# A first expert layer whose second biases move from TensorE to VectorE, with the shared expert's transposition ahead of the third down projection

## The reference, cut to what matters

```python
xf = x.reshape(-1, h)
scores = jax.nn.sigmoid(xf @ gate_w.T + gate_b)
top_scores, top_idx = jax.lax.top_k(scores, TOP_K)
top_scores = top_scores / (top_scores.sum(-1, keepdims=True) + 1e-06)
comb = (jax.nn.one_hot(top_idx, E, dtype=xf.dtype) * top_scores[..., None]).sum(1)
hdn = jax.nn.gelu(jnp.einsum('th,ehf->etf', xf, w1) + b1[:, None, :], approximate=False)
y = jnp.einsum('etf,efh->eth', hdn, w2) + b2[:, None, :]
routed = jnp.einsum('te,eth->th', comb, y)
shared = (jax.nn.gelu(xf @ sw1 + sb1, approximate=False) @ sw2 + sb2) * 0.1
return (routed + shared).reshape(b, s, h)
```

## Time and profile before

| | |
|---|---|
| timed runs | 260.24, 260.38, 261.11 us; median 260.38 |
| profiled execution, its own time | 262.31 us |
| its span, first to last instruction | 260.5 us |
| TensorE, weight loads | 232.2 us (89%), 142.5 us (55%) |
| VectorE, ScalarE | 169.2 us (65%), 153.2 us (59%) |
| GpSimd | 45.3 us (17%) |
| mean granted clock of TensorE | 0.967 |

### The profile page before, as it was taken

How to read it: one execution, slowest core, us unless ns; L and a number is a source line. 1 busy time by engine, 2 the same in 40 slices (tenths; PEclk the granted TensorE clock), 3 DMA queues, 4 the chain that set the end, 5 groups by cost and what they waited for, 6 DMA issues and landing times.

```text
span 260.5 us, 5274 instructions
## 1 busy us (share of the span) xinstructions
PE 232.2 (89%) x2100; PEld 142.5 (55%) x2100; DVE 169.2 (65%) x419; ACT 153.2 (59%) x260; POOL 45.3 (17%) x72
## 2 busy tenths in 40 slices
PE   7799979399999988999889999999999998888875
PEld 2333325399754434367587666666666666542335
DVE  4598997999933254633764878778787780144571
ACT  6669986966825974825376556665566656500140
POOL 8885994000000010000310000000000000000120
PEclk9999999779999999999999999999999999968997
DMA  5999102000909000004999999979999896600000
GB/s 128 227 321 431 75 0 84 0 0 10 356 0 357 8 0 0 0 3 62 99 138 104 125 100 129 115 103 118 98 112 107 101 114 200 292 3 0 1 1 5
DMA packets 5663, 26.88 MB, mean 103 GB/s; under 512 B 2083, under 2 KB 2628, under 8 KB 3942
## 3 DMA queue, kind: packets, MB, share of 16 engines
q1 hardware_dynamic: 5638, 26.54, 52.9%
HBM read 16.84 MB, written 0.03 MB: 65 GB/s over the span
## 4 chain that ended last, share of the span: by engine, by line
PE 60%; DVE 17%; ACT 10%; POOL 4%; DMA 4%; issue 3%; POOLq 1%; SPq 0%; DVEq 0%
PE B L1116 32%; PE A L1116 22%; DVE mid L759 4%; ACT probs L657 4%; DMA ctxT<-in_ctxT 4%; ACT probs L567 1%; DVE top L768 1%; POOL ctxT L380 1%; DVE mid L775 1%; PE B L1344 1%; DVE probs L846 1%; POOL rstd L377 1%; PE B L1459 1%; PE A L1161 1%; PE A L1224 1%
## 5 line engine op out<-in xcount | busy, mean ns | idle before, releaser
L1000 DVE TENSOR_REDUCE mx<-B 128x1 f32<-128x512 f32 (+1 forms) x104 | 65.0, 656 | 17.6 <-PE B L1116 17.0
L657 ACT ACTIVATE probs<-A 128x896 f32<-128x896 f32 x56 | 50.6, 917 | 26.7 <-PE A L1116 26.4
L377 POOL TENSOR_TENSOR rstd<-ve,mhalf 64x1 f32<-64x1 f32 x9 | 5.2, 574 | 188.7 <-DVE ve L694 181.9
L1116 PE MATMUL B<-probs,scores 128*32 128x128 f32 x736 | 34.0, 280 | 2.5 <-ACT probs L657 2.5
L1116 PE MATMUL B<-scores,moe_w 128*128 128x512 bf16 (+1 forms) x96 | 26.0, 354 | 0.4 <-DVE mx L1000 0.4
L1116 PE MATMUL A<-ctxT,qq 97*128 97x512 f32 (+1 forms) x52 | 22.8, 582 | 2.3 <-DMA ctxT<-in_ctxT 1.6
L1116 PEld LDWEIGHTS B<-probs,scores 128*32 128x32 f32 x736 | 19.0, 109 | 10.0 <-ACT probs L657 5.8
L759 DVE MAX8 mid<-scores 128x8 f32<-128x196 f32 x64 | 17.7, 348 | 3.0 <-ACT scores L492 3.0
L1116 PEld LDWEIGHTS A<-ctxT,qq 97*128 97x128 f32 x52 | 9.3, 189 | 16.1 <-issue 7.4
L846 DVE SCALAR_TENSOR_TENSOR probs<-scores,top,probs 128x512 f32<-128x512 f32 (+1 forms) x26 | 17.5, 716 | 0.1
L492 ACT ACTIVATE scores<-A 128x512 f32<-128x512 f32 (+1 forms) x26 | 13.9, 576 | 5.2 <-PE A L1116 5.0
(11 more groups left out here) (374 smaller groups left out, 372.0 us busy)
## 6 DMA issues: line engine op xcount, KB each, us to landing
ctxT<-scores SPq DMA_DIRECT2D x20, 148.0 KB, 4.7
ctxn<-in_ctxn SPq DMA_DIRECT2D x1, 2352.0 KB, 19.3
moe_w<-in_moe_w SPq DMA_DIRECT2D x1, 2304.0 KB, 8.5
ctxn<-in_moe_w SPq DMA_DIRECT2D x1, 2304.0 KB, 9.2
scores<-in_e_gu SPq DMA_DIRECT2D x1, 2048.0 KB, 8.7
ctxn<-scores SPq DMA_DIRECT2D x10, 148.0 KB, 4.6
moe_w<-scores SPq DMA_DIRECT2D x10, 148.0 KB, 4.8
blob_m<-in_blob_m SPq DMA_DIRECT2D x1, 1467.0 KB, 14.4
```

Source lines behind the costliest of these rows:

```text
L377: nc.gpsimd.tensor_tensor(rstd[:, :], ve[:, :], mhalf[0:T, :], ALU.pow).then_inc(S["rstd_ready"], 1)
L657: A_(probs[:, (n % RING) * 1024:(n % RING) * 1024 + w], A[:, 2 * (n % 2):2 * (n % 2) + 2, :].rearrange("p a b -> p (a b)")[:, 0:w], ACT.Ex ...
L1000: V.tensor_reduce(mx[:, m, t:t + 1], bank[:, 0:SB0[t][1]], AX_X, ALU.max).then_inc(S["max_used"], 1)
L1116: return mm(out_, lhsT, rhs, start=start, stop=stop)
```

## The change

The second biases of the eight experts leave TensorE. A tile `pair_b2` holds them, for each pair the two biases repeated over the 64 tokens of the two halves (128 x 512). VectorE adds bias x `csel` to the sum in four instructions (`add_bias`, to `acc` 2 and 3). The tile takes the place of `wcf`, whose tile becomes `wide` with 128 partitions, and is loaded once the film matmul has read `wcf`. The shared expert's bias stays on TensorE and goes ahead of the wait for Gelu. The four spins of the layer go, and the loop is written out, with transposition 4 directly behind transposition 3, ahead of down projection 2.

```diff
-SPIN = {"c2T": 2, "c2": 2, "cT": 1, "hT": 2, "ut": 3, "g1": 2, "vT": 2, "turn": 1, "down": 1, "x3": 3}
+SPIN = {"c2T": 2, "c2": 2, "cT": 1, "hT": 2, "ut": 3, "g1": 2, "vT": 2, "x3": 3}
...
-ROWS = {0: {"film_b": 4 * D, "film_1": 4 * D, "out_b": D}, 32: {"moe_b2": 9 * D},
+ROWS = {0: {"film_b": 4 * D, "film_1": 4 * D, "out_b": D}, 32: {"sb2": D},
...
-        wcf = sb("wcf", [DC, 4 * D])
+        wide = sb("wide", [P, 4 * D])
+        wcf = wide[0:DC, :]
+        pair_b2 = wide[:, :].rearrange("p (a d) -> p a d", d=D)
...
             sp.dma_start(moe_w2, dram["moe_w2"]).then_inc(S["ld_w2"], 16)
+            sp.wait_ge(S["film_ps"], 1)
+            sp.dma_start(wide[:, :], dram["pair_b2"]).then_inc(S["ld_small"], 16)
...
-            prev = add_pair(0, x2w[:, :], "moe_y_ps")
+
+            def add_bias(p, at, prev):
+                link(V.scalar_tensor_tensor(acc[:, at, :], pair_b2[:, p, :], csel[:, p:p + 1], prev, ALU.mult, ALU.add))
+                return acc[:, at, :]
+
+            dve.wait_ge(S["ld_small"], 32)
+            prev = add_bias(0, 2, x2w[:, :])
+            prev = add_bias(1, 3, prev)
+            prev = add_pair(0, prev, "moe_y_ps")
             moe_pre(2)
+            prev = add_bias(2, 2, prev)
             prev = add_pair(1, prev, "moe_y_ps")
             moe_pre(3)
+            prev = add_bias(3, 3, prev)
             moe_pre(4)
...
             def moe_down(p):
-                pe.wait_ge(S["moe_gelu"], p + 1)
                 if p >= 2:
                     pe.wait_ge(S["moe_acc"], p - 1)
                 ne = 2 if p < 4 else 1
                 y = [B[2 + p % 2][e * T:(e + 1) * T, 0:D] for e in range(2)]
-                for e in range(ne):
-                    one(y[e], one_at["moe_b2"][:, 0:T], W["moe_b2"][:, (2 * p + e) * D:(2 * p + e + 1) * D], stop=False)
+                if p == 4:
+                    one(y[0], one_at["sb2"][:, 0:T], W["sb2"], stop=False)
+                pe.wait_ge(S["moe_gelu"], p + 1)
...
-                                   moe_w2[:, (4 * (2 * p + e) + c) * D:(4 * (2 * p + e) + c + 1) * D], start=False, stop=(c == 3))
+                                   moe_w2[:, (4 * (2 * p + e) + c) * D:(4 * (2 * p + e) + c + 1) * D],
+                                   start=(c == 0 and p < 4), stop=(c == 3))
...
-            for p in range(5):
-                moe_turn(p)
-                if p + 2 < 5:
-                    moe_up(p + 2)
-                else:
-                    spin("turn", A[:, 3, :])
-                if p == 1:
-                    pe.wait_ge(S["ld_w2"], 16)
-                if p >= 1:
-                    moe_down(p - 1)
-                if p >= 3:
-                    spin("down", A[:, 3, :])
+            moe_turn(0)
+            moe_up(2)
+            moe_turn(1)
+            moe_up(3)
+            pe.wait_ge(S["ld_w2"], 16)
+            moe_down(0)
+            moe_turn(2)
+            moe_up(4)
+            moe_down(1)
+            moe_turn(3)
+            moe_turn(4)
+            moe_down(2)
+            moe_down(3)
             moe_down(4)
```

More of the change, by code:

```diff
@@ L107 @@
 tokT_ps tokT_sb norm_ready k_ps k_hi k_rest k_mid k_left k_low
-ld_x ld_a ld_s ld_m ld_l ld_rows ld_gmask ld_mask ld_ctx ld_dft ld_w1 ld_w2 ld_e6 out_stored
+ld_x ld_a ld_s ld_m ld_l ld_rows ld_small ld_mask ld_ctx ld_dft ld_w1 ld_w2 ld_e6 out_stored
 const_ready var_ready rstd_ready mask_row
@@ L315, in _ @@
             sp.dma_start(blob["blob_x"][:, :], dram["blob_x"]).then_inc(S["ld_x"], 16)
-            sp.dma_start(gmask, dram["gmask"]).then_inc(S["ld_gmask"], 16)
+            sp.dma_start(gmask, dram["gmask"]).then_inc(S["ld_small"], 16)
             sp.dma_start(blob["blob_s"][:, :], dram["blob_s"]).then_inc(S["ld_s"], 16)
@@ L477, in _ @@
             A_(ctxT[DC:P, ones_cuts[2]:], onec[DC:P, 0:1].to_broadcast([P - DC, n]), ACT.Copy).then_inc(S["mask_row"], 1)
-            act.wait_ge(S["ld_gmask"], 16)
+            act.wait_ge(S["ld_small"], 16)
             A_(mask_f, gmask, ACT.Copy, scale=-NEG, bias=NEG).then_inc(S["mask_row"], 1)
@@ L554, in _ @@
                     act.wait_ge(S["wcf_ps"], 1)
-                    A_(wcf[:, :], A[0:DC, 2, :], ACT.Copy).then_inc(S["wcf_sb"], 1)
+                    A_(wcf, A[0:DC, 2, :], ACT.Copy).then_inc(S["wcf_sb"], 1)
                     keys_at("flag")
@@ L1262, in _ @@
             pe.wait_ge(S["wcf_sb"], 1)
-            one(B[3][0:T, :], cT[:, :], wcf[:, :], start=False).then_inc(S["film_ps"], 1)
+            one(B[3][0:T, :], cT[:, :], wcf, start=False).then_inc(S["film_ps"], 1)
             project_keys("film")
@@ L1641, in lay_out @@
     w["moe_b1T"] = np.concatenate([m0["b1"].reshape(32, P), m0["sb1"].reshape(4, P)], 0).T
-    w["moe_b2"] = np.concatenate([m0["b2"].reshape(-1), m0["sb2"]])
+    w["sb2"] = m0["sb2"]
     w["wq1"], w["bq1"] = x1["Wq"], col(x1["bq"])
@@ L1672, in lay_out @@
     out["dft_k"] = w["dft_k"]
+    out["pair_b2"] = np.repeat(m0["b2"].reshape(4, 2, D).transpose(1, 0, 2).reshape(2, -1), T, 0)
     out["fill"] = np.concatenate([np.full((1, G // 2), 0x3F803F80, np.uint32), np.zeros((15, G // 2), np.uint32)], 0).view(np.float32)
```

## The result

The changed kernel takes 259.46 us in the median of 12 runs (257.92 to 261.23); the kernel before, run beside it, 260.72 us (12 runs, 259.8 to 262.52). The ratio is 0.9936 [0.9908, 0.9964]: 1.7 us faster, between 0.9 and 2.4; the two medians alone are 1.26 us apart. The forecast was 2.04 us and 258.3; taken from 260.72 it would be 258.7. The profiled execution has a span of 257.1 us and a time of its own of 258.88.

What follows compares the result with a forecast made beforehand. The prediction took TensorE alone to bound the first expert layer; biases 1.45 plus spins 0.76 minus a new wait of 0.17 gave 2.04 us, from 260.38 to 258.3 us. Range 257.3 to 259.6, inner range 258.0 to 258.8.

Steps and rivals of the forecast that it cites:

- The bound: In the first expert layer TensorE alone forms the chain, 109.74 to 120.2 us, so work leaving it shortens the program.
- The bias matmuls: Four pairs of bias matmuls leave TensorE's down projections in the first expert layer, 0.36 us each, saving 1.45 us.
- The spins: Four spin matmuls leave TensorE in the first expert layer, 0.11, 0.21, 0.22 and 0.22 us, saving 0.76 us.
- The order of transposition 4: Transposition 4 (0.39 us) ahead of down projection 2 by itself costs and gives nothing on TensorE.
- The new wait for Gelu 3: TensorE waits for Gelu ahead of down projection 3, costing 0.17 us, with bounds of 0.05 and 0.3.
- VectorE and the load: VectorE's four bias instructions cost 0 on the path, 0.1 us at worst; the 256 KB bias load costs nothing.
- The sum: Biases, spins and the new wait in the expert layer: 1.45 + 0.76 - 0.17 = 2.04 us, giving 258.3 us.
- The whole program: Everything behind the first expert layer moves up by what the layer gives, 2.04 us, from 260.38 to 258.3 us.
- Gelu binds harder: Down projection 3 waits 0.6 to 1.2 us, or pair 3's sum comes late; time 259.0 us; chance 0.12.
- The change gives nothing: TensorE's saved time is waited away at the loads or on VectorE; time stays 260.4 us; chance 0.03.
- Slower by a clock fall in the layer: Low clock in the expert layer from transposition 3 on costs 3.0 us, giving 261.4 us; chance 0.05.
- The tail's clock changes: The program's shift changes the tail's low-clock stretches: 256.8 us (0.08) or 259.8 us (0.10); chance 0.18 in all.

Runs made afterwards that it cites:

- e1: The changed kernel with the old loop and its four spins back, biases still on VectorE; 259.92 us, ratio to the kernel before 0.9914, layer 11.13 us.
- e2: The kernel before with the new loop order and without the four spins, biases kept on TensorE; 260.98 us, ratio to the kernel before 0.9969, layer 12.13 us.
- e8: The changed kernel with the bias tile's load issued behind transposition 1 instead of the film product; 260.18 us, ratio to the kernel before 0.9949, layer 11.21 us.
- e3: The changed kernel with transposition 4 back behind down projection 2, still without spins; 259.67 us, ratio to the kernel before 0.9904, layer 10.62 us.
- e4: The changed kernel with each of VectorE's four bias instructions issued twice; 259.71 us, ratio to the kernel before 0.9897, layer 10.62 us.
- e5: The kernel before with more fill matmuls in three places to hold the clock up; 261.28 us, ratio to the kernel before 0.9960, layer 12.88 us.
- e6: The changed kernel with more fill matmuls in three places to hold the clock up; 259.60 us, ratio to the kernel before 0.9899, layer 10.62 us.
- e10: The changed kernel with Gelu 3 in halves and the shared expert's bias off TensorE too; 259.14 us, ratio to the kernel before 0.9908.
- e7: The changed kernel with Gelu 3 cut into two instructions of 256 columns; 259.55 us, ratio to the kernel before 0.9921, layer 10.41 us.

## Why the prediction was right, and where its sizes were off

**The bound: right.** TensorE alone set the layer's length before, so work taken from it shortened the program; e1 and e2 show it for each kind of work by itself.

**The bias matmuls: the mechanism right, the term too small.** Forecast 4 x 0.36 = 1.45, measured 1.75 (e1). The 0.36 was the distance from the bias's weight load to the next one. It holds for pairs 2 and 3 (0.37 each) and misses 0.15 each at pairs 0 and 1. The row to see is 109.20 in the timeline after: the weight loads of the first chunk stand there 0.41 us before their product (109.61), under the up projection, while in the earlier trace rows those of the first real product stood at 110.03, behind the bias. At unit 4 even two products of down projection 1 (0.11 us) stand between the two parts of the up projection. The bias rows had kept the first real weights from being fetched under the up projection. The same gain was there to be had at pair 3, directly behind down projection 2 (0.51 by e8), and the wait for Gelu 3 hid it. The Trainium skill (TensorE: Matmul & The Clock Gate, Part 2: What happens when you issue a matmul, Step-by-step: what each phase is for) has TensorE take weight loads ahead of matmuls under way while the matmuls keep their order. For the loads the trace agrees, 0.41 us ahead; for the order of the matmuls its records do not, since two products of down projection 1 (111.51 in the chain) stand between the two records of up projection 4 (111.24 and 111.65), which comes first in the program. That a bias in front prices this at 0.15 us a pair, only the rows show.

**The spins: right.** Forecast 0.76, measured 0.75 (e2).

**The order of transposition 4: right**, worth nothing (e3).

**The new wait for Gelu 3: right in place, its cost too small.** Forecast 0.17 with bounds 0.05 and 0.3. The idle time of TensorE in front of down projection 3 is 0.18, as forecast. Its cost is 0.24 as the difference between the parts and the whole, and 0.40 against a down projection 3 that starts without waiting (e8 against the changed kernel). The path itself was well read: forecast 0.68 + 0.69 + 0.03 + 0.63 + 0.15 = 2.18 from the start of transposition 3 to that of down projection 3, measured 115.30 - 113.12 = 2.18. What was off is that a wait was priced at its idle time. The 28 records behind it take 2.69 us, against 1.02 + 1.59 = 2.61 for the same ones in e1 and 0.88 + 1.59 = 2.47 in e8: the weight loads that would have run ahead under down projection 2 had to wait too.

**VectorE and the load: right**, both cost nothing (e4), and the load has its price when it comes late (e8). The first sum was forecast at 110.9 and stood at 110.85.

**The sum.** 1.75 + 0.75 - 0.24 = 2.26 in the layer against the forecast's 2.04: the bias term was 0.30 too small, the wait 0.07 too small and the spins 0.01 too large. The x3 product was forecast near 117.4 and stood at 117.17; SyncE's first stack copy near 118.2, at 118.02.

**The whole program.** The forecast let all that follows move up by what the layer gives. That is what the timings say within their scatter (0.9919, give or take 0.0014, against 0.9913), though the first of them alone was low. The range, 257.3 to 259.6, holds the 259.46, but only just, and there is luck in it. The forecast's own inner range, 258.0 to 258.8, missed; what held the time is the upper part, put in for a rival that did not come true. Of the 1.1 us over 258.3, 0.34 is the kernel before, whose median was 260.72 beside this one and not the 260.38 that the forecast was counted from; the rest is that the two medians differed by 1.26 in this first timing, where all five timings together give 2.1.

**The rivals.** *Gelu binds harder* (0.6 to 1.2 us): out, a wait of 0.18 and a cost of 0.24 to 0.40. *The change gives nothing*: out. *Slower by a clock fall in the layer*: out; the granted clock was 1.00 there in all 13 profiles, with the two transpositions together (e2) and apart. (The 4.5 us of low clock that this rival names is where the gain would be used up; by its own figures 261.2 takes 6.3.) So the rule of the Trainium skill on transpositions (TensorE: Matmul & The Clock Gate, Part 4: PE-mode transpose) was not seen to have any effect on this stretch; transpositions here never stood for more than 0.98 us without other matmuls, and longer rows of them weren't tried. *The tail's clock changes*: not with the change, but from execution to execution. Three profiles of the changed kernel have their low stretches at 228.25 (6.8 us), at 229.25 and 239.5 (3.4 each), and at 227.5 (6.8); e2 and e5 have no stretch at 253.5 like the one of before, and e4, which has the change, has one at 250.75. It made the pair of spans differ by 3.4 us. The price put on the 6.7 us stretch, about 1.5 us on the path, was near the 1.7 that before and e5 show. By the means over the runs, before and after have the same granted clock, 0.97.

**What stays open.** By the times, up to some 0.5 us of the 2.26 may be lost behind the layer, though in the three profiles of the changed kernel it was whole 110 us later. In e4, e6 and e10 the clock fell right behind it (from 124.5, 124.25 and 122.75 on, 3.4 us each), and the way from the transposition of the normalised x3 to the first exponentials of the second attention on ScalarE took 18.9 to 19.1 us in place of 18.2 to 18.3; in the other ten profiles it didn't. All three of these have the shorter layer, but the same instructions stand there in every kernel, and three profiles are too few to tie it to the change. In e7 some 0.7 to 0.8 us were lost within the attention with the clock at 1.00 throughout, for a reason that was not looked for.

## What to carry to other kernels

Where one engine is busy without a gap, price each piece of work on it by its length in the chain, and then look at what stands in front of it: a small matmul with weights of its own between two long stages also costs the overlap of the next stage's weight loads, here 0.15 us on top of 0.37. When work is taken from such an engine, follow the path over the other engines that it used to cover, with the shortened times; two savings that are each free of waits can share one wait when both are made (1.75 + 0.75 gave 2.26). Look at the row of weight loads as well as at that of the products: a wait costs more than its idle time (0.40 for 0.18 here), and products without a gap (e7) do not mean that nothing waits. And where spans of two single profiles differ, cut them at fixed instructions first: the stretch of the change repeated to 0.01 us, the spans didn't to 1 us.

## What had not been expected of the hardware

- The same program has its clock fall at other places in each execution: in three profiles of the changed kernel the low stretches in the tail begin at 228.25, at 229.25 and 239.5, and at 227.5. The time from the start to transposition 0, of the same instructions in all of them, varied from 106.16 to 107.49 us.
- Much less time at the low level gave little: in e5 some 9 us less of it, for about 1 us [0.2, 1.9] in the whole runs, though the one stretch of some 6.8 us that can be compared by itself cost 1.7.
- A wait of 0.18 us for the data of a weight load cost 0.40, since the loads that would have run ahead under the products before (e8) had to wait as well; and in e7 the products show no gap while the loads do.
- The 256 KB load took 8.2 us to land when issued behind the 2304 KB one and 2.7 us when nothing else was under way (e8).
